# A windowed-attention and mixture-of-experts block on one core: choice, statistics and weight loads moved

## The reference

```python
x = x + attention(ln(x), eps 1e-6)          # softmax over the row, and over the column, of 16 places each
t = tokens(x); n = ln(t, eps 1e-5)
logits = n @ wg                              # 256 x 8 experts
idx = argmax(softmax(logits)); mask = one_hot(idx)
loc = cumsum(mask, axis=0) - 1               # place in the expert's queue, 256 places each
gate = softmax(logits)[idx] * (loc < 256)
h = relu(gathered(n) @ w1[e])                # 256 x 1024, 8 experts
out = t + gate * scattered(h @ w2[e])        # 1024 x 256
```

## Time and profile before

| | us |
|---|---|
| three runs | 195.95, 196.92, 197.92 (median 196.92) |
| the profiled execution | 195.56 |
| its span (first to last instruction) | 193.6 |
| PE busy | 177.0 (91%) |
| DVE, POOL, ACT busy | 128.5 (66%), 116.5 (60%), 113.1 (58%) |
| mean granted clock of TensorE | 0.963 |

### The profile page before, as it was taken

The page is one execution under the profiler, slowest core; times in us unless marked ns, Lnnn a source line. Parts: engine busy times, 40 slices in busy tenths (PEclk is TensorE's granted clock), DMA queues, the critical chain, the costliest instruction groups (busy, mean ns, idle before and its releaser), DMA issues.

```text
span 193.6 us, 3843 instructions
## 1 busy us (share of the span) xinstructions
PE 177.0 (91%) x1344; PEld 169.4 (88%) x1344; DVE 128.5 (66%) x394; ACT 113.1 (58%) x272; POOL 116.5 (60%) x138
## 2 busy tenths in 40 slices
PE   7989959999999998989999990999999999999980
PEld 7969848999999996779999980999999999999980
DVE  0669998597797798758766518558477583765520
ACT  3369841967967777524677167195691947929100
POOL 5263982375876776084149247667686966768462
PEclk9999966999999999999999996699999999999999
DMA  5899994111311213684961571924909449061010
GB/s 170 198 369 362 278 333 195 45 56 56 112 60 67 97 60 110 179 288 133 332 237 55 163 270 35 339 118 114 357 19 319 172 129 331 24 226 40 0 69 27
DMA packets 23588, 31.67 MB, mean 164 GB/s; under 512 B 2456, under 2 KB 20377, under 8 KB 23568
## 3 DMA queue, kind: packets, MB, share of 16 engines
q1 hardware_dynamic: 20832, 26.38, 41.5%
q0 software_dynamic: 1648, 4.24, 6.5%
q10 hardware_dynamic: 1088, 0.79, 1.4%
HBM read 23.02 MB, written 8.55 MB: 163 GB/s over the span
## 4 chain that ended last, share of the span: by engine, by line
PE 73%; DVE 9%; ACT 5%; issue 4%; POOL 4%; DMA 3%; POOLq 1%; DVEq 0%; ACTq 0%
PE banks_o L641 9%; PE banks_v L571 7%; PE banks_v L572 7%; PE banks_v L578 7%; PE bank_q L578 4%; PE bank_q L571 3%; PE bank_q L572 3%; DMA w_in_sb<-in_L_ffn_w 3%; PE bank_s L571 3%; PE bank_s L578 3%; PE bank_s L572 3%; POOL w_low L517 2%; PE bank_xT L685 2%; PE bank_xT L571 2%; PE bank_pT L578 2%
## 5 line engine op out<-in xcount | busy, mean ns | idle before, releaser
L517 POOL TENSOR_TENSOR w_low<-w_in_sb,w_high 128x1024 fp32r<-128x1024 f32 x15 | 35.9, 2411 | 10.7 <-ACT w_high L903 10.5
L903 ACT ACTIVATE w_high<-w_in_sb 128x1024 fp32r<-128x1024 f32 x30 | 30.3, 1051 | 5.9 <-DMA w_in_sb<-in_L_ffn_w 5.9
L534 POOL DMA_INDIRECT out<-y,goal x16 | 16.2, 1012 | 13.9 <-DVE y L1276 8.3
L478 POOL DMA_INDIRECT slots<-row,slot x14 | 14.6, 1043 | 16.5 <-DVE slot L1166 8.1
L1254 DVE TENSOR_TENSOR w_low<-w_in_sb,w_high 128x1024 fp32r<-128x1024 f32 x12 | 17.6, 1501 | 3.4 <-ACT w_high L903 3.4
L641 PE MATMUL banks_o<-v_sb,pT 128*128 128x266 f32 x64 | 18.0, 429 | 0.0
L1262 DVE SCALAR_TENSOR_TENSOR h_low<-bank_s,h_high 128x512 fp32r<-128x512 f32 x8 | 5.5, 689 | 16.6 <-ACT h_high L997 16.6
L997 ACT ACTIVATE h_high<-bank_xT 128x512 fp32r<-128x512 f32 x8 | 4.8, 598 | 19.6 <-PE bank_xT L578 17.5
L571 PE MATMUL banks_v<-w_high,h_high 128*128 128x256 f32 x64 | 16.0, 287 | 0.0
L572 PE MATMUL banks_v<-w_high,h_low 128*128 128x256 f32 x64 | 15.7, 283 | 0.0
L524 POOL TENSOR_SCALAR var_g<-ss_g 128x2 f32<-128x2 f32 x8 | 6.1, 765 | 14.3 <-ACT pT L977 8.2
(11 more groups left out here) (244 smaller groups left out, 640.0 us busy)
## 6 DMA issues: line engine op xcount, KB each, us to landing
w_in_sb<-in_L_ffn_w SPq DMA_DIRECT2D x16, 1024.0 KB
sl<-slots SPq DMA_DIRECT2D x9, 266.0 KB, 4.3
slots<-empty SPq DMA_DIRECT2D x8, 266.0 KB, 8.4
out<-row SPq DMA_DIRECT2D x7, 256.0 KB, 2.3
sl<-in_x SPq DMA_DIRECT2D x4, 256.0 KB, 6.9
sl<-in_x SPq DMA_DIRECT2D x2, 512.0 KB, 9.2
table_in<-in_tables SPq DMA_DIRECT2D x1, 294.0 KB, 7.5
w_in_sb<-in_L_conv_Wk SPq DMA_DIRECT2D x1, 256.0 KB, 3.4
```

Of the source, the lines that this page charges most:

```text
L478: nc.gpsimd.indirect_dma_start(slot_rows, bass.IndirectOffsetOnAxis(ap=slot_of(i)[:, t:t + 1].bitcast(u32), axis=0), row_of(i)[:, t, :], N ...
L517: step = nc.gpsimd.tensor_tensor(w2_low[e % 2][:, half, :], w2_in_sb[:, half, :], w2_high[e % 2][:, half, :].bitcast(f32), ALU.subtract)
L534: nc.gpsimd.indirect_dma_start(out_rows, bass.IndirectOffsetOnAxis(ap=goal[j][:, c:c + 1].bitcast(u32), axis=0), y[j][:, c, :], None, boun ...
L903: nc.scalar.activation(high[e % 2][:, half, :], raw[:, half, :], ACT.Copy).then_inc(ready, 1)
```

## The change

What moves, part by part:

1. **Turns.** DVE chooses the expert of batch i-2 after `maxima(i)` in turn i (before: of i-1 at the turn's end), and `place` and `to_slot` come after `query_low`. On PE the counts stand behind `attention_out`, and for batches 0 to 4 they are written into `bank_pT` in place of a corner of `ps_v`; `transpose_prob` waits for their reading in place of `values`.
2. **Statistics.** `first_norm(4)` goes into turn 1, the two halves of group 5 into turns 2 and 3. GpSimd waits for `weights(0)` ahead of its first residual sum, and makes `first_rstd(5)` in its fourth round.
3. **Dispatch.** Each half of `ps_x0` is finished before the next, ScalarE writes the first half's `high`, DVE the second's. `xn2_low` moves ahead of the last `place`.
4. **Weights.** w2 is loaded in two halves with a semaphore each; SP issues w1(e+1) ahead of w2(e). ScalarE makes the `high` of w2(e+1) after the hidden quarters, the exponentials and the squares of slots, and of w1(e+2) in two pieces around the last hidden quarter. DVE follows with `split_w1`. GpSimd splits w2(1) ahead of the first scatter, and `slot_rstd(e+1)` stands ahead of `split_w2(e+1)`.

```diff
-        ps_count = halves(ps_v[:, 0, MW:MW + 2 * E])
-        ps_count_late = halves(bank_xT[:, 0:2 * E])
+        ps_count, ps_count_fifth, ps_count_late = (halves(a) for a in (bank_pT[:, 0:2 * E], ps_v[:, 0, MW:MW + 2 * E], bank_xT[:, 0:2 * E]))
...
+        def count_of(i):
+            return ps_count if i < EARLY - 1 else ps_count_fifth if i < EARLY else ps_count_late
+        w2_half = [slice(h * FC // 2, (h + 1) * FC // 2) for h in range(2)]
...
             sp.wait_ge(m_ready, 1)
-            sp.dma_start(w2_in_sb[:, :, :], w2_view[0]).then_inc(w2_in, 16)
+            for h in range(2):
+                sp.dma_start(w2_in_sb[:, w2_half[h], :], w2_view[0][:, w2_half[h], :]).then_inc(w2_in[h], 16)
...
-            sp.wait_ge(w2_split, 1)
-            sp.wait_ge(first_w2_low, 1)
-            sp.dma_start(w2_in_sb[:, :, :], w2_view[1]).then_inc(w2_in, 16)
+            def load_w2(e, h):
+                sp.wait_ge(w2_low_ready[h], e)
+                sp.dma_start(w2_in_sb[:, w2_half[h], :], w2_view[e][:, w2_half[h], :]).then_inc(w2_in[h], 16)
+            load_w2(1, 1)
+            load_w2(1, 0)
             for e in range(2, E):
-                sp.wait_ge(w2_split, e)
-                sp.dma_start(w2_in_sb[:, :, :], w2_view[e]).then_inc(w2_in, 16)
                 if e < E - 1:
                     sp.wait_ge(w1_split, e + 1)
                     sp.dma_start(w1_in_sb[:, :, :], w1_view[e + 1]).then_inc(w1_in, 16)
+                load_w2(e, 0)
+                load_w2(e, 1)
... (GpSimd)
             pool.wait_ge(b_ready, 1)
+            pool.wait_ge(u_ready, 2)
             x_and_bias(0)
...
             x_and_bias(1)
-            first_rstd(5)
             for i in range(2, B):
...
+                if i == 3:
+                    first_rstd(5)
                 scatter_rows(i - 2)
...
             split_w2(0, [0])
             slot_rstd(0)
-            slot_rstd(1)
+            split_w2(1, range(2))
             scatter_y(0)
-            split_w2(1, range(2))
+            slot_rstd(1)
             for e in range(1, E - 1):
+                slot_rstd(e + 1)
                 split_w2(e + 1, range(2))
-                slot_rstd(e + 1)
                 scatter_y(e)
... (PE)
+                wait(pe, count_read, min(i, EARLY) - 1)      # in transpose_prob
...
                 query(i + 1)
+                attention_out(i - 1, 0)
+                attention_out(i - 1, 1)
                 if i > 1:
                     counts(i - 2)
-                attention_out(i - 1, 0)
-                attention_out(i - 1, 1)
                 values(i)
...
             for c in range(DC):
                 dispatch(1, c)
-            for c in range(DC):
                 dispatch_low(c)
... (PE, expert_out)
-                pe.wait_ge(w2_split, e + 1)
+                for h in range(2):
+                    pe.wait_ge(w2_low_ready[h], e + 1)
... (ScalarE, experts)
             for e in range(1, E - 1):
-                hidden(e + 1, [0, 1])
-                split_w2(e + 1)
-                hidden(e + 1, [2, 3])
+                hidden(e + 1, [0, 1, 2])
+                if e + 2 < E:
+                    split_w1(e + 2, [0])
+                hidden(e + 1, [3])
                 if e + 2 < E:
                     gathered_T(e + 2)
+                    split_w1(e + 2, [1])
                 slot_exps(e)
-                if e + 2 < E:
-                    split_w1(e + 2)
                 slot_squares(e + 1)
+                split_w2(e + 1)
... (VectorE, turn)
                 maxima(i, 1)
+                if i > 1:
+                    choose(i - 2)
                 if i == 1:
-                    first_norm(5)
-                else:
-                    place(i - 2)
-                    to_slot(i - 2)
+                    first_norm(4)
+                elif i == 2:
+                    dve.wait_ge(x_in[5], 16)
+                    first_stats(12, 14)
+                elif i == 3:
+                    first_stats(14, 16)
+                    first_shares(5)
                 weights(i, 0)
                 weights(i, 1)
                 query_low(i + 1)
+                if i > 1:
+                    place(i - 2)
+                    to_slot(i - 2)
                 residual(i - 1, 0)
                 residual(i - 1, 1)
-                choose(i - 1)
... (VectorE, ahead of the turns)
-            first_norm(4)
             for i in range(1, B - 1):
                 turn(i)
+            choose(B - 3)
```

More of the change, by code:

```diff
@@ L512, in split_w2 @@
             def split_w2(e, parts):
[L514 to L518, removed]
+                for h in parts:
+                    pool.wait_ge(w2_high_ready, 2 * e + h + 1)
+                    half = w2_half[h]
+                    nc.gpsimd.tensor_tensor(w2_low[e % 2][:, half, :], w2_in_sb[:, half, :], w2_high[e % 2][:, half, :].bitcast(f32),
+                                            ALU.subtract).then_inc(w2_low_ready[h], 1)
             def slot_rstd(e):
@@ L616, in values @@
                 wait(pe, v_ready, i)
-                if 0 in which:
-                    wait(pe, count_read, i - 1)
+                if i == B - 1 and 0 in which:
+                    pe.wait_ge(count_read, i - 1)
                 for t in which:
@@ L642, in attention_out, with counts @@
                 step.then_inc(o_made, 1)
-            def counts(i, late=False):
+            def counts(i):
                 pe.wait_ge(chosen_ready, i + 1)
@@ L648, in counts @@
                 wait(pe, count_read, i)
-                if not late:
+                if i == EARLY - 1:
                     pe.wait_ge(v_ready, i + 2)
-                ps, b = ps_count_late if late else ps_count, before[i % 2]
+                ps, b = count_of(i), before[i % 2]
                 nc.tensor.matmul(ps[:, 0, :], upper, chosen[:, 0, :], start=True, stop=False)
@@ L744, in _ @@
             transpose_prob(B - 1)
-            counts(B - 2, late=True)
+            counts(B - 2)
             attention_out(B - 1, 0)
@@ L772, in _ @@
                 dispatch(0, c)
-            counts(B - 1, late=True)
+            counts(B - 1)
             dispatch_early()
@@ L895, in second_w1_high, with split_w1, split_w2 @@
                 nc.scalar.activation(w1_high[1][:, c, part], w1_in_sb[:, c, part], ACT.Copy).then_inc(w1_high_ready, 1)
-            def split_w(high, loaded, raw, ready, e, which=range(2)):
-                act.wait_ge(loaded, 16 * (e + 1))
-                parts = raw.shape[1] // 2
-                for part in which:
-                    half = slice(part * parts, (part + 1) * parts)
-                    nc.scalar.activation(high[e % 2][:, half, :], raw[:, half, :], ACT.Copy).then_inc(ready, 1)
-            def split_w1(e, **which):
-                split_w(w1_high, w1_in, w1_in_sb, w1_high_ready, e, **which)
-            def split_w2(e, **which):
-                split_w(w2_high, w2_in, w2_in_sb, w2_high_ready, e, **which)
+            def split_w1(e, which=range(2)):
+                act.wait_ge(w1_in, 16 * (e + 1))
+                for c in which:
+                    nc.scalar.activation(w1_high[e % 2][:, c, :], w1_in_sb[:, c, :], ACT.Copy).then_inc(w1_high_ready, 1)
+            def split_w2(e, which=range(2)):
+                for h in which:
+                    act.wait_ge(w2_in[h], 16 * (e + 1))
+                    nc.scalar.activation(w2_high[e % 2][:, w2_half[h], :], w2_in_sb[:, w2_half[h], :], ACT.Copy).then_inc(w2_high_ready, 1)
             act.wait_ge(fold_a, 1)
@@ L964, in _ @@
                 centred(sl_early, xs[0], t).then_inc(xs0_ready, 1)
-            for c in range(DC):
-                act.wait_ge(x0_made, c + 1)
-                step = nc.scalar.activation(xg_high[0][:, c, :], ps_x0[c], ACT.Copy)
-            step.then_inc(gT_ready, 1)
+            act.wait_ge(x0_made, 1)
+            nc.scalar.activation(xg_high[0][:, 0, :], ps_x0[0], ACT.Copy).then_inc(gT_ready, 1)
             def slot_squares(e):
@@ L1045, in first_norm @@
                 nc.vector.tensor_scalar(var_eps[:, a:b], mean_var[:, a:b, 1], EPS_C, None, ALU.add).then_inc(var_ready, 1)
+            def first_norm(g):
+                dve.wait_ge(x_in[g], 16)
+                first_stats(*X_GROUPS[g])
+                first_shares(g)
             def low_part(low, exact, high):
@@ L1221, in _ @@
             choose(B - 1)
-            place(B - 1)
-            onehots(1)
             for t in range(2):
@@ L1227, in _ @@
                                                xn2[1][:, t, :].bitcast(f32), ALU.add, ALU.subtract).then_inc(xn2_low_ready, 1)
+            place(B - 1)
+            onehots(1)
             to_slot(B - 1)
@@ L1281, in _ @@
             first_w2_piece(2)
-            for c in range(DC):
-                dve.wait_ge(gT_ready, 1)
+            dve.wait_ge(x0_made, 2)
+            nc.vector.tensor_copy(xg_high[0][:, 1, :], ps_x0[1]).then_inc(x1_high_ready, 1)
+            for c, high_ready in enumerate((gT_ready, x1_high_ready)):
+                dve.wait_ge(high_ready, 1)
```

42 lines of the change are left out of this document (22 added, 20 removed).

## The result

The changed kernel is slower, not faster: 199.47 us median of four runs (199.33 to 202.62) against 196.80 of four runs of the kernel before (195.95 to 197.92). The ratio is 1.0149, 95% interval 1.0086 to 1.0211. (Some executions of any kernel here come out over 1.5% slower than its fastest; the medians hold them, the ratios and intervals leave them out, so a ratio isn't always the quotient of two medians.) The profiled execution took 199.33 us, span 197.2. PE's busy time is the same, 177.1 us; DVE's has grown from 128.5 to 137.8 us, though part 3 gives it only one eviction of 0.4 us more to do; 6.6 us of the growth lie ahead of the first expert, hidden(0). The forecast was 188.6 us.

The account below looks back on a forecast made before the run. PE, busy 91% of the span, bounds the kernel with its work, pauses and half-clock stretches. Terms summed to -7.55 us from the profiled 195.56, giving 188.0; 188.6 us after moving halfway toward the runs' median. Range 184.6 to 191.8.

Parts of the forecast that it names:

- Turn 1: PE's wait for xT_low in turn 1 and the half clock behind it go: 5.85 us saved.
- Small waits in turns 1 to 3: Late query_low makes PE wait a little in turns 1 to 3: 0.4 us charged, bounds 0 and 2.5.
- Turns 2 to 6: nothing: Moving choose and place on DVE in turns 2 to 6 stays hidden by PE's queue: no cost.
- `place` goes to where the counts are long made: In turns 2 to 6, DVE's place after query_low finds its counts ready; part of the zero-cost claim.
- Dispatch: Ahead of the first expert, evicting one half beside the second's products gains 0.6 us (0.3 to 0.8).
- First experts: PE waits 1.2 us ahead of hidden(2), behind ScalarE's w2(1) halves; bounds 0 and 2.5.
- granted clock 1.00 from 20 to about 165: Sign of being right: in the changed profile PE keeps full clock over this stretch, in us.
- Stall at w1(3): Ahead of hidden(3), the 5.4 us wait and 1.8 us of clock go: 7.2 us saved.
- Last expert: Ahead of out(7), a new pause of 2.7 us for GpSimd's w2(7) halves, plus 1.8 us of half clock.
- three signs of being wrong: Out(7) does not wait, a clock fall stands in the turns, or any out(2) to out(6) waits for w2.
- B: Rival: the pause moves within turns 1 to 3, clock falls again, 5.85 us comes back: 194.5 us; chance 0.07.
- C: Rival, slower: experts 2 to 6 overrun a 2.1 us margin; pauses from about 1.5 us cost more clock; chance 0.04.

Follow-up runs that it names:

- e2: Changed kernel with GpSimd's four low pieces of w1(1) moved out of turns 3 to 6, behind the last pre_residual: 196.00 us, ratio 0.9957.
- e9: Kernel of e5 with ScalarE's w2(1) split also moved later, plus GpSimd's residual sum waiting for DVE's choice of the batch before: 184.29 us, ratio 0.9369.
- e3: Kernel before with part 1 (turn order) alone: 203.57 us, ratio 1.0367.
- e1: Changed kernel with part 1 (turn order) alone undone: 193.95 us, ratio 0.9877 to the kernel before.
- e12: Kernel before with part 2 (statistics spread over turns 1 to 3, GpSimd waiting for weights(0)) alone: 196.59 us, ratio 0.9915.
- e11: Changed kernel with GpSimd's residual sum, from turn 2 on, waiting for DVE's weights of the same batch: 200.10 us, ratio 1.0191.
- e8: Kernel of e1 with ScalarE's w2(1) split later, and PE awaiting w2's low halves only ahead of out(e)'s third pass: 186.61 us, ratio 0.9501.
- e4: Kernel before with part 4 (weights) alone: 195.19 us, too scattered for an interval; 193.53 us in the profiled execution.
- e5: Kernel of e1 with the last expert's w2 split earlier on ScalarE, and on GpSimd ahead of slot_rstd(7): 190.42 us, ratio 0.9655.
- e10: Kernel of e5 with ScalarE's w2(1) split also moved later, plus choice of batch 0 behind xT_low in turn 2: 186.80 us, ratio 0.9520.

## Why the prediction was wrong, point by point

- **Turn 1, -5.85 us.** Right: the third `transpose_x` begins at 28.37 in place of 33.76, -5.4, with the granted clock at 1.00.
- **Small waits in turns 1 to 3, +0.4.** The first two turns show none. Turn 3 has the held `both`, 1.66 us.
- **"Turns 2 to 6: nothing".** This is the step that failed. `choose` was said to fill a gap, by its 1.2 us of undisturbed length; it was not asked what runs on GpSimd in that gap. From the third `transpose_x` to hidden(0) the kernel lost 8.4 us: 4.4 for `qT_low`, 1.2 for `chosen`, 1.4 for the tokens of the first expert, and 1.4 in short pieces. The text had the rule and the rows, and used them on `minus_mean` in one turn only the earlier trace rows. By the same rule `both` and `ratio`, moved to where GpSimd's pair lies, had to be priced at up to 2.6 us each. And "`place` goes to where the counts are long made" looked at what `place` waits for, not at what waits for `place`: GpSimd's scatters, and the pair behind them. e2, e9 and e3 show the holding from three sides. Not all of the 8.4 us is part 1's: with it undone (e1) 3.1 us stay, with part 2 alone (e12) 3.35, where GpSimd's sum holds the choice at a turn's end.
- **Dispatch, -0.6.** Nothing came: hidden(0) still waits 0.6 us, for DVE's half in place of ScalarE's.
- **First experts, +1.2.** The wait was 1.86 us, inside the bounds, and the clock's fall behind it, which I had not charged, cost about 1.7 (4 us at a mean of 0.62 and 4 at 0.95: 4 x 0.43), against the sign "granted clock 1.00 from 20 to about 165".
- **Stall at w1(3), -7.2.** Right. From hidden(2) to out(7) the kernel before took 78.46 us, the changed one 75.70 with 2.45 of new wait and 1.7 of clock in it: -6.9. No expert waits for w2 from 2 to 6.
- **Last expert, +2.7 and +1.8.** Right: 2.45 us of wait, and from the start of out(7) to the last `y` 7.44 us where it took 5.96, so 1.5 of clock.

None of the three signs of being wrong came: out(7) waited, no clock fall stood in the turns, and no out(e), e = 2 to 6, waited for w2. They didn't cover several waits of 0.6 to 1.7 us in a row. One reading was off without weight: a granted clock of 0.85 in the slice 25 to 26 puts the fall at 25.70, not at 25.85, with PE idle at either.

Up to hidden(0) the sum had -6.05 us and the trace +3.0: 9.0 of the 11.3 us between 188.0 and 199.33; most of the rest is the clock at the first experts. Of the rivals, B named the right place, a pause that comes back in the turns, but put it into turns 1 to 3 and gave it 0.07, since it looked for one long pause with its clock and not for a small toll in each turn. The slower rival, C, did not occur. Its "from about 1.5 us" for the length of pause that costs clock is shown by no run; what the runs have is in the last section.

By parts, alone in the kernel before: part 1 +3.7%, part 2 -0.9%, part 4 -1.0% in the profiled execution (four runs too scattered for an interval). Part 3 was not run alone. The sum, +1.8%, is near the whole's +1.5%, nearer than the intervals can tell.

## What to carry to other kernels

A move on VectorE is priced by what GpSimd does at the new place: list for both engines what overlaps, and mark the VectorE operations whose operands are all in SBUF, the smallest too, since their length is then that of GpSimd's work. Keep GpSimd's long operations beside reads of PSUM, if need be by making GpSimd wait (e9, -1.1% by one line, across two chips and with intervals that just overlap); such a wait has to be placed by the same list, since in e11 it only moved the holding to other operations. Ask also what waits for an operation that is moved back. And put a wait where the operand is first read, not at the head of the product (e8, -2.1%).

## What was not expected of the hardware

- A held VectorE operation can stay held through more than one GpSimd operation: two (2.57, 2.49, 2.10 us) and four in a row (4.82 us). In e11 the hold ended between the two of a pair, in four turns out of four. What decides this is open.
- A cast of two numbers per partition with one operand (`slot`, 1.14 us in e11) was held too. The Trainium skill, "SBUF — State Buffer", section "Who interferes with whom", names casts among the operations that can contend; the trace agrees (1.14 us, ended with GpSimd's `low`).
- The same pause need not draw the clock down. Ahead of out(7), 2.45 us long in six executions, it fell in four (0.57 over the next 4 us in the changed kernel) and stayed at 1.00 in two (e2, e4). Ahead of hidden(2) a pause of 1.86 us drew a fall in the changed kernel and none in e11. From 20 us on, single waits of 1.77 us and less drew none, one of 1.92 (e11) and one of 2.26 (e5) did, as did those of 2.45 in turn 1 and of 4.2 us and more each time; but at the start of e10, e11, e12 and e3 the clock fell behind a wait of only 1.15, 1.12, 0.82 and 0.37 us, and in e9 behind none that the profile shows. So the length of the last pause alone doesn't tell. The falls ahead of out(7) and hidden(2) cost the changed kernel 1.5 and 1.7 us, so part of the scatter of one kernel's times may be this; that was not shown.
